# A three-layer graph network on one core: the slot table scattered three columns a step, and the first weights rounded earlier

## Chip, cores and metric

One core of a Trainium2 chip. The metric is the device time of one execution in microseconds (us); lower is better. Engines: PE (TensorE), DVE (VectorE), ACT (ScalarE), POOL (GpSimd) and SP (SyncE, which here only issues DMAs).

## The reference, cut to what matters

```python
x = x + gnn(layernorm(x), src, dst)       # x is 10000 x 512 f32, 10000 edges sorted by dst
x = x + ffn(layernorm(x))                 # 8 experts of 64 hidden columns, top 2
# gnn, three times:
h_neigh = segment_sum(h[src], dst) / max(deg, 1)
h = relu(h @ W_self[l] + h_neigh @ W_neigh[l] + b[l]);  h = h / |h|
```

## The kernel before, in words

All products are done with both factors split into two float16 parts (high and low, three matmuls for each pair of 128-blocks; `products`, L487). A weight matrix is rounded once: ACT writes the high part (`weight_hi`, L835), DVE the low part (`weight_lo`, L1095). Both need the matrix's scale, which comes from column norms (`square_sums` on PE, `weight_norm` and `weight_scale` on DVE, `largest_norm` on POOL).

**The first layer** goes over the 10000 nodes in their own order, in 79 tiles of 128. For tile t: SP loads x (L551); DVE takes mean and variance (`stats0`); POOL raises the variance to -1/2 (`dev0`, L674); DVE normalises (`norm0`, L1224); ACT and DVE make the high and low parts (`hi0`, `lo0`); PE turns the tile (`turn`); ACT copies it from PSUM (`turn0`, L871, HT); PE multiplies by the neighbour weights (`neigh`, psY) and by the own weights (`own`, psS); ACT and DVE write the first result as two halves (`yhi`, `ylo`), DVE adds the bias to the second (`sev`); SP stores both (L562, L564), 256 KB each. The second and third layers go over 79 tiles of edges instead and need tables: for each slot (tile, column) the node that it belongs to.

**The order of work.** Every engine runs its own list of steps. `run_plan` (L117) goes through the steps; in each, first the jobs that are set to this step run, then the stages in the order listed, each on tile step + offset. A stage with offset 4 works four tiles ahead. POOL's stage is `dev0` with offset 4, so in step s it serves tile s + 4. PE's stages are `neigh` at 0, `turn` at 1 and `own` at 0, and `own(t)` waits until `sev(t-1)` has emptied the accumulator. ACT's are `hi0` at 2, `yhi` at 0, `turn0` at 1; so `turn0` of tile t stands behind `hi0` of tile t + 1, and PE's tile t waits for the power of tile t + 1. DVE's are `sev` at -1, `norm0` at 2, `stats0` at 4, `lo0` at 2, `ylo` at 0.

**The tables** are made beside this as jobs. In steps 4 to 23 POOL scatters the node table, four columns a step. DVE works out each node's slot (to step 46). **From step 48 on POOL scatters the slot table in DRAM**: 80 columns, each an indirect DMA that writes 125 rows of 8 bytes (`columns`, L650, the DMA at L653), four a step in steps 48 to 67, each step's after `dev0`. Columns of even and odd steps count on two semaphores, s_scat0 and s_scat1, 16 for each column that has landed. Before a step's columns, POOL waits until those of two steps before have landed (`slot_columns`, L692). In step 68 `slot_columns_done` (L702) waits for all and loads the table back (L705), ahead of that step's `dev0`. DVE copies it in step 71 (`slot_table_loaded`, L1297), PE turns it in step 72 (`turn_slots`, L1627), DVE makes the index tables in step 73 (`tables`, L1302, s_tables at its end). After the first layer POOL and PE wait for s_tables, and POOL for the landing of all rows stored, before the gathers of the second layer start (`gather`, L728).

**The first weights.** Matrix 0 (n0) is rounded on ACT and DVE in step -1, matrix 1 (s0) in step 0. SP's `load_weight(2)` and `load_weight(3)` (L501, steps -1 and 0) wait for the low parts of 0 and 1.

Of the kernel before, what the change touches and what calls it, by code (L numbers as in the profile page):

```python
# [26 lines left out]
NP_, NF = 80, N // 80  # L27
# [5 lines left out]
STEP_EDGES = 4  # L33
STEP_INFO = STEP_EDGES + 20
STEP_SLOTS = 28
STEP_SCATTER = 48
STEP_TABLES = 71
NODES_A_STEP = 7
X_RING = 4

# [1 line left out]
def WSTEP(m):  # L42

    return 2 + 4 * (m - N_FIRST) + (m == 6)
# [60 lines left out]
def run_steps(tiles, stages, begin, end, run=0):  # L105
    for step in range(begin, end):
        for off, f in stages:
            if 0 <= step + off < tiles:
                f(Tile(step + off, run))
# [6 lines left out]

def run_plan(tiles, stages, jobs, windows=()):  # L117
    offs = [o for o, _ in stages]
    begin, end = -max(max(offs), 0), tiles - min(min(offs), 0)
    cuts = sorted({begin, end} | {j[0] for j in jobs} | {e for w in windows for e in w[:2]})  # L120
    for a, b in zip(cuts, cuts[1:]):
        for at, f, arg in jobs:
            if at == a:
                f() if arg is None else f(arg)
        run_steps(tiles, stages + [(0, f) for x, y, f in windows if x <= a and b <= y], a, b)
# [105 lines left out]
def build(nc, x, src, dst, W_self, W_neigh, b, Wg, W1, b1, W2, b2, ln_g, ln_b, out_g, out_b, out):  # L231
    with ExitStack() as ctx:
# [6 lines left out]
        def sem(name):  # L239
            return ctx.enter_context(nc.semaphore(name))  # L240

        def dram(name, shape, dt):
            return nc.dram_tensor(name, shape, dt)
# [6 lines left out]
        table = dram("slot_table", [SLOTS, 2], F32)  # L250
# [122 lines left out]
        s_sc = [sem(f"s_scat{i}") for i in range(2)]  # L373
# [8 lines left out]
        def view(at, parts, n, dt=F32):  # L382
            v = area[0:parts, at:at + n]
            return v if dt is F32 else v.bitcast(dt)
# [19 lines left out]
        slotT = view(P * 9, P, 80, U32)  # L404
        ndT = view(P * 10, P, 160).rearrange("p (t two) -> p t two", two=2)
# [93 lines left out]
        def _(sp):  # L499
# [58 lines left out]
            def store(t):  # L558
# [5 lines left out]
                sp.dma_start(Sd0[bass.ds(t.t * P, rows), :], SB[t.slot(2)][0:rows, :]).then_inc(s.s2[t.slot(2)], 16)  # L564

            run_plan(TN, [(5, load_x), (-1, store)],
                     [(-2, small_loads, None), (-2, table_starts, None), (-1, load_weight, 2), (0, load_weight, 3)]
                     + [(WSTEP(m - 1) + 1, load_weight, m) for m in range(4, len(NAMES))])
# [47 lines left out]
        def _(pool):  # L616

            node_limit = pool.alloc_register("node_limit")
            slot_limit = pool.alloc_register("slot_limit")
# [30 lines left out]
            def columns(index, value, to, limit, rows, i, at, count):  # L650

                for k in range(at, at + count):
                    pool.indirect_dma_start(  # L653
                        to[:, :], bass.IndirectOffsetOnAxis(ap=index[0:rows, k:k + 1], axis=0),
                        value[0:rows, k, :], None, bounds_check=limit, oob_is_err=False).then_inc(s_sc[i], 16)
# [31 lines left out]
            def info_done():  # L687
                for i in range(2):
                    pool.wait_ge(s_sc[i], 640)
                pool.dma_start(nI, info.rearrange("(p k) two -> p k two", p=NP_)).then_inc(s_nload, 16)  # L690

            def slot_columns(t):  # L692

                g = t + -STEP_SCATTER
                i = t.slot(2)
                pool.wait_ge(s_sc[i], (g + -2).landed(2) * 4 + 640)
                columns(slotT, ndT, table, slot_limit, NF, i, g.t * 4, 4)

            def slot_columns_in():
                pool.wait_ge(s_scat_in, 2)  # L700

            def slot_columns_done():  # L702
                for i in range(2):
                    pool.wait_ge(s_sc[i], 1280)
                pool.dma_start(tI, table.rearrange("(p k) two -> p k two", p=T)).then_inc(s_tload, 16)  # L705

            run_plan(TN, [(4, dev0)],
                     [(WSTEP(m) + 2, largest_norm, m) for m in range(N_FIRST, len(NAMES))]
                     + [(STEP_GATE + 2, largest_norm, CG), (STEP_EDGES, edge_columns_in, None), (STEP_INFO, info_done, None),
                        (STEP_SCATTER, slot_columns_in, None), (STEP_SCATTER + 20, slot_columns_done, None)],  # L710
                     [(STEP_EDGES, STEP_INFO, info_columns), (STEP_SCATTER, STEP_SCATTER + 20, slot_columns)])
            pool.wait_ge(s_tables, 1)

            for l in (1, 2, 3):
# [3 lines left out]
                tiles = TN if l == 1 else T  # L718
# [99 lines left out]
        def _(act):  # L818
# [39 lines left out]
            def yhi(t, l):  # L858
                i = t.slot(2)
                s = ph[l]  # L860
                act.wait_ge(s.y, (t + 1).n)
                if t.t >= 2:
                    act.wait_ge(s.ys[i], (t + -2).landed(2))
                k = Y_LN / (WUP * LN_UP) if l == 0 else Y_H / (WUP * H_UP)
                act.activation(YB[i][:, 0:D], psY[i][:, :], ACT.Copy, scale=k).then_inc(s.yhi, 1)  # L865

            def turn0(t):
# [4 lines left out]

            rest = range(N_FIRST, len(NAMES))
            run_plan(TN, [(2, hi0), (0, lambda t: yhi(t, 0)), (1, turn0)],
                     [(-1, weight_hi, 0), (0, weight_hi, 1)] + [(WSTEP(m) + 4, weight_hi, m) for m in rest]
                     + [(WSTEP(m), squares, m) for m in rest] + [(STEP_GATE, gate_squares, None)])

            def carry_hi(t, l):
# [109 lines left out]
        def _(dve):  # L988
# [252 lines left out]
            def ylo(t, l):  # L1241
                s = ph[l]
                i = t.slot(2)
                dve.wait_ge(s.yhi, (t + 1).n)
                k = Y_LN / (WUP * LN_UP) if l == 0 else Y_H / (WUP * H_UP)
                dve.scalar_tensor_tensor(YB[i][:, D:2 * D], psY[i][:, :], k, YB[i][:, 0:D], ALU.mult, ALU.subtract  # L1246
                                         ).then_inc(s.ylo, 1)

            def sev(t, l):
                s = ph[l]  # L1250
                i = t.slot(2)
                dve.wait_ge(s.sp, (t + 1).n)
                if t.t >= 2:
                    dve.wait_ge(s.s2[i], (t + -2).landed(2))
                c = C[f"s{l}"]
                dve.scalar_tensor_tensor(SB[i][:, :], psS[i][:, :], downs[:, c:c + 1], bias[:, l, :],  # L1256
                                         ALU.mult, ALU.add).then_inc(s.sev, 1)
# [44 lines left out]
            def tables():  # L1302
# [6 lines left out]
                for l in range(LAYERS):  # L1309
# [6 lines left out]
            rest = range(N_FIRST, len(NAMES))  # L1316
            run_plan(TN,
                     [(-1, lambda t: sev(t, 0)), (2, norm0), (4, stats0), (2, lo0), (0, lambda t: ylo(t, 0))],
                     [(-3, weight_norm, 1), (-2, weight_scale, 1), (-1, weight_lo, 0), (0, weight_lo, 1),
                      (0, self_down, None), (1, bias_columns, None), (1, edges, None), (3, edges_turned, None)]  # L1320
                     + [(WSTEP(m) + 2, weight_norm, m) for m in rest] + [(WSTEP(m) + 3, weight_scale, m) for m in rest]
                     + [(WSTEP(m) + 5, weight_lo, m) for m in rest]
# [6 lines left out]
                        (STEP_SLOTS, node_ranks, None), (STEP_SLOTS + FREE_STEPS, slots_by_node, None),  # L1329
                        (STEP_SCATTER - 1, slots_turned, None), (STEP_TABLES, slot_table_loaded, None),  # L1330
                        (STEP_TABLES + 2, tables, None)],
                     [(STEP_SLOTS, STEP_SLOTS + FREE_STEPS, free_slots)])
# [236 lines left out]
        def _(pe):  # L1569
# [96 lines left out]
            def own(t, l):  # L1666
# [3 lines left out]
                if l == 0 and t.t == 0:  # L1670
# [6 lines left out]
                        (STEP_SLOTS - 1, counts_before, None), (STEP_SCATTER - 2, turn_nodes, None),  # L1677
                        (STEP_TABLES + 1, turn_slots, None)])

# [116 lines left out]
```

## Time and profile before

| | |
|---|---|
| median of 3 runs | 2206.17 us (2205.99 to 2208.15) |
| profiled execution | 2204.11 us, its span 2202.1 us |
| PE busy | 2037.8 us, 93% of the span |
| DVE, ACT, POOL busy | 1721.8, 994.8, 1262.6 us |
| granted TensorE clock, mean | 0.968 of full |
| first layer | to about 533 us of the span |

The span runs from the first instruction to the last. The profiled execution took 2.0 us more than its span, and is 2.1 us below the median. In the rows, times count from the span's start. "idle 1.31 <-DMA x" says that the engine sat idle for 1.31 us before the instruction and that the end of this was set by the DMA x. "issue" means that nothing that the profile shows was waited for.

### The profile page before, as it was taken

How to read it: one execution, taken by the hardware profiler on the slowest of the kernel's cores; microseconds unless marked ns; L12 is line 12 of the kernel's file. 1: busy time of each engine (PE TensorE's matmuls, PEld its weight loads, DVE VectorE, ACT ScalarE, POOL GpSimd, SP SyncE). 2: the span in 40 equal slices, each digit the busy share in tenths (PEclk: the TensorE clock that was granted, in tenths of full speed). 3: DMA queues.
4: the chain of work that ended last, by engine and by line, in shares of the span. 5: the costliest groups of instructions: out<-in, count | busy, mean ns of one | idle time of the engine just before them, and what ended most of it. 6: DMA issues, size and time to landing. Idle time of an engine off the chain costs nothing.

```text
span 2202.1 us, 43921 instructions
## 1 busy us (share of the span) xinstructions
PE 2037.8 (93%) x15309; PEld 1138.2 (52%) x15315; DVE 1721.8 (78%) x4122; ACT 994.8 (45%) x1699; POOL 1262.6 (57%) x1396
## 2 busy tenths in 40 slices
PE   6999999877999999997999999997399999999997
PEld 2444444333444444443444444443077777777775
DVE  7768985444788888885888888885589999999984
ACT  4444333223333433442333433443566666766741
POOL 2784127752566665553444444443668888888854
PEclk9999999998999999998999999998599999999998
DMA  6664349863555555553666666664668888888853
GB/s 203 165 162 132 130 135 130 103 103 98 163 173 174 174 174 174 175 175 134 200 216 219 216 219 218 218 218 164 169 146 173 181 173 176 178 176 172 177 88 43
DMA packets 246210, 364.12 MB, mean 165 GB/s; under 512 B 115578, under 2 KB 115752, under 8 KB 245992
## 3 DMA queue, kind: packets, MB, share of 16 engines
q1 hardware_dynamic: 185175, 195.88, 35.0%
q0 software_dynamic: 60816, 165.43, 28.8%
q8 instruction: 125, 2.05, 0.4%
q14 instruction: 94, 0.76, 0.1%
HBM read 175.81 MB, written 165.31 MB: 155 GB/s over the span
## 4 chain that ended last, share of the span: by engine, by line
PE 74%; POOL 7%; DVE 6%; issue 5%; DMA 3%; ACT 3%; SPq 0%; DVEq 0%; POOLq 0%; ACTq 0%
PE psS L492 29%; PE psY L492 23%; PE psY L1730 10%; POOL slot_table L653 4%; PE psT L1654 4%; PE psA L1698 2%; PE psA L1699 2%; POOL node_info L653 2%; PE psS L1754 1%; DMA slot_table<-area 1%; DVE R L1364 1%; DVE area L1408 1%; PE psY L1732 1%; PE psA L1764 1%; POOL scl L674 1%
## 5 line engine op out<-in xcount | busy, mean ns | idle before, releaser
L492 PE MATMUL psY<-w_n,HT 128*128 128x512 f16 x2844 | 663.8, 384 | 45.4 <-ACT HT L871 43.1
L492 PE MATMUL psS<-w_s,HT 128*128 128x512 f16 x2844 | 652.6, 379 | 0.0
L492 PEld LDWEIGHTS psY<-w_n,HT 128*128 128x128 f16 x2844 | 278.3, 99 | 394.8 <-ACT HT L871 55.1
L492 PEld LDWEIGHTS psS<-w_s,HT 128*128 128x128 f16 x2844 | 268.3, 98 | 280.5
L898 ACT ACTIVATE RR<-R 128x512 f32<-128x512 f32 x237 | 149.5, 631 | 362.5 <-DVE R L1364 362.5
L757 POOL DMA_INDIRECT y_rows<-YB,poutT x158 | 160.4, 1015 | 188.2 <-DVE YB L1246 159.9
L750 POOL TENSOR_TENSOR scl<-ssm,halfpow 128x1 f32<-128x1 f32 x158 | 88.6, 560 | 247.7 <-DVE ssm L1382 247.7
L492 PE MATMUL psS<-w_w,raw 128*128 128x512 f16 x948 | 217.4, 379 | 0.0
L1256 DVE SCALAR_TENSOR_TENSOR SB<-psS,downs,bias 128x512 f32<-128x512 f32 x237 | 177.6, 749 | 47.5 <-PE psS L492 41.1
L1246 DVE SCALAR_TENSOR_TENSOR YB<-psY,YB 128x512 f16<-128x512 f32 x237 | 162.4, 685 | 36.5 <-ACT YB L865 36.1
L906 ACT ACTIVATE HH<-RR,scl 128x512 f16<-128x512 f32 x158 | 114.0, 722 | 148.7 <-POOL scl L750 148.7
L1364 DVE SCALAR_TENSOR_TENSOR R<-psA,invs,Sl 128x512 f32<-128x512 f32 x237 | 173.3, 731 | 9.8 <-ACT G L887 8.6
L728 POOL DMA_INDIRECT G<-y_rows,srcT x120 | 136.1, 1134 | 62.8 <-issue 31.4
L865 ACT ACTIVATE YB<-psY 128x512 f16<-128x512 f32 x237 | 137.8, 581 | 75.3 <-PE psY L492 56.1
L856 ACT ACTIVATE HH<-R 128x512 f16<-128x512 f32 x79 | 49.7, 630 | 269.2 <-DVE R L1224 267.3
L1654 PEld LDWEIGHTS psT<-iden,HH 128*128 128x128 f16 x1896 | 126.8, 98 | 67.6 <-ACT HH L906 7.1
L807 POOL DMA_INDIRECT out_dram<-raw,poutT x79 | 147.0, 1861 | 15.5 <-issue 14.3
L1654 PE MATMUL psT<-iden,HH 128*128 128x128 f16 x1896 | 146.1, 221 | 10.0 <-DVE HH L1231 4.6
L674 POOL TENSOR_TENSOR scl<-ssm,halfpow 128x1 f32<-128x1 f32 x79 | 62.2, 789 | 160.7 <-DVE ssm L1217 155.1
L492 PEld LDWEIGHTS psS<-w_w,raw 128*128 128x128 f16 x948 | 91.6, 97 | 109.2
L728 POOL DMA_INDIRECT area<-y_rows,srcT x117 | 123.3, 1054 | 30.8 <-issue 30.8
L1349 DVE SCALAR_TENSOR_TENSOR G<-psA,G 1x512 f16<-1x512 f32 x78 | 52.9, 679 | 93.7 <-ACT G L887 93.7
(280 smaller groups left out, 3657.0 us busy)
## 6 DMA issues: line engine op xcount, KB each, us to landing
self_rows<-SB SPq DMA_DIRECT2D x236, 256.0 KB, 2.0
Sl<-self_rows SPq DMA_DIRECT2D x158, 256.0 KB, 3.9
area<-in_x_dram SPq DMA_DIRECT2D x78, 256.0 KB, 4.8
y_rows<-YB SPq DMA_DIRECT2D x78, 256.0 KB, 4.3
out_dram<-obb SPq DMA_DIRECT2D x78, 256.0 KB, 4.2
raw<-in_L_gnn_W_neigh_dram SPq DMA_DIRECT2D x12, 256.0 KB
raw<-in_L_gnn_W_self_dram SPq DMA_DIRECT2D x12, 256.0 KB, 4.2
y_rows<-YB,poutT POOLq DMA_INDIRECT x158, 3.0
```

Of the source, the lines that this page charges most:

```text
L492: mm = eng.matmul(acc, lhs[:, a, c, :], w[:, bpart, c, :], start=(n == 0), stop=(stop and n == 3 * KC - 1))
L653: pool.indirect_dma_start(to[:, :], bass.IndirectOffsetOnAxis(ap=index[0:rows, k:k + 1], axis=0), value[0:rows, k, :], None, bounds_check= ...
L728: pool.indirect_dma_start(G[i][:, :], None, Yd[l - 1][:, :], bass.IndirectOffsetOnAxis(ap=srcT[:, t.t:t.t + 1], axis=0), bounds_check=node ...
L757: pool.indirect_dma_start(Yd[l][:, :], bass.IndirectOffsetOnAxis(ap=poutT[:, t.t:t.t + 1], axis=0), YB[i][:, :], None, bounds_check=node_l ...
L807: pool.indirect_dma_start(out[:, :], bass.IndirectOffsetOnAxis(ap=poutT[:, t.t:t.t + 1], axis=0), OUT[i], None, bounds_check=node_limit, o ...
L865: act.activation(YB[i][:, 0:D], psY[i][:, :], ACT.Copy, scale=k).then_inc(s.yhi, 1)
L898: act.activation(RR[i][:, :], R[i][:, :], ACT.Relu).then_inc(s.rr, 1)
L1246: dve.scalar_tensor_tensor(YB[i][:, D:2 * D], psY[i][:, :], k, YB[i][:, 0:D], ALU.mult, ALU.subtract).then_inc(s.ylo, 1)
L1256: dve.scalar_tensor_tensor(SB[i][:, :], psS[i][:, :], downs[:, c:c + 1], bias[:, l, :], ALU.mult, ALU.add).then_inc(s.sev, 1)
L1364: dve.scalar_tensor_tensor(R[i][:, :], psA[0 if l == 3 else i][:, :], invs[:, l - 1, t.t:t.t + 1], Sl[i][:, :], ALU.mult, ALU.add).then_in ...
L1654: mm = pe.transpose(psT[i][:, a, c, :], HH[i][:, a, c * P:(c + 1) * P], iden16[:, :])
L1730: pe.matmul(psH[:, cols], w[:, bpart, c, cols], h[:, a, c, :], start=first, stop=False)
```

## The change

The slot table's columns go out three a step over 27 steps (48 to 74, two columns in the last) instead of four over 20. What POOL waits for before a step's columns is the same, those of two steps before. `slot_columns_done` moves from step 68 to 75, `slot_table_loaded` on DVE from 71 to 78, `turn_slots` on PE from 72 to 79, `tables` from 73 to 80. Step 79 is behind PE's last stage and step 80 behind DVE's, so `run_plan` now runs on until the last job. `weight_hi` of matrices 0 and 1 moves on ACT from steps -1 and 0 to -2 and -1, `weight_lo` of matrix 0 on DVE from step -1 to -2; that of matrix 1 stays in step 0.

```diff
-STEP_TABLES = 71
+SLOTS_A_STEP = 3
+SCATTER_STEPS = -(-80 // SLOTS_A_STEP)
+STEP_TABLES = 78
...
 def run_plan(tiles, stages, jobs, windows=()):
     offs = [o for o, _ in stages]
-    begin, end = -max(max(offs), 0), tiles - min(min(offs), 0)
+    begin, end = -max(max(offs), 0), max([tiles - min(min(offs), 0)] + [j[0] + 1 for j in jobs])
...
+            def slots_sent(g):
+
+                return sum(min(SLOTS_A_STEP, 80 - SLOTS_A_STEP * k) for k in range(g % 2, g, 2))
+
             def slot_columns(t):
 
-                g = t + -STEP_SCATTER
-                i = t.slot(2)
-                pool.wait_ge(s_sc[i], (g + -2).landed(2) * 4 + 640)
-                columns(slotT, ndT, table, slot_limit, NF, i, g.t * 4, 4)
+                g = (t + -STEP_SCATTER).t
+                at = g * SLOTS_A_STEP
+                pool.wait_ge(s_sc[g % 2], 640 + 16 * slots_sent(g))
+                columns(slotT, ndT, table, slot_limit, NF, g % 2, at, min(SLOTS_A_STEP, 80 - at))
...
             def slot_columns_done():
                 for i in range(2):
-                    pool.wait_ge(s_sc[i], 1280)
+                    pool.wait_ge(s_sc[i], 640 + 16 * slots_sent(SCATTER_STEPS + (SCATTER_STEPS + i) % 2))
                 pool.dma_start(tI, table.rearrange("(p k) two -> p k two", p=T)).then_inc(s_tload, 16)
...
-                        (STEP_SCATTER, slot_columns_in, None), (STEP_SCATTER + 20, slot_columns_done, None)],
-                     [(STEP_EDGES, STEP_INFO, info_columns), (STEP_SCATTER, STEP_SCATTER + 20, slot_columns)])
+                        (STEP_SCATTER, slot_columns_in, None), (STEP_SCATTER + SCATTER_STEPS, slot_columns_done, None)],
+                     [(STEP_EDGES, STEP_INFO, info_columns), (STEP_SCATTER, STEP_SCATTER + SCATTER_STEPS, slot_columns)])
...
-                     [(-1, weight_hi, 0), (0, weight_hi, 1)] + [(WSTEP(m) + 4, weight_hi, m) for m in rest]
+                     [(-2, weight_hi, 0), (-1, weight_hi, 1)] + [(WSTEP(m) + 4, weight_hi, m) for m in rest]
...
-                     [(-3, weight_norm, 1), (-2, weight_scale, 1), (-1, weight_lo, 0), (0, weight_lo, 1),
+                     [(-3, weight_norm, 1), (-2, weight_scale, 1), (-2, weight_lo, 0), (0, weight_lo, 1),
```

## Rows read from the trace of the kernel before

**Rows 1.** The page: the chain that ended last, shares of the span by line

```profile
PE psS L492 29%; PE psY L492 23%; PE psY L1730 10%; POOL slot_table L653 4%; PE psT L1654 4%; PE psA L1698 2%; PE psA L1699 2%; POOL node_info L653 2%; PE psS L1754 1%; DMA slot_table<-area 1%; DVE R L1364 1%; DVE area L1408 1%; PE psY L1732 1%; PE psA L1764 1%; POOL scl L674 1%
```

**Rows 2.** Busy time of each engine by stage, clock, DMA share, GB/s

```profile
core 0: us, PE busy (x) PEld busy (x) DVE busy (x) ACT busy (x) POOL busy (x), PEclk, DMA share, GB/s
324.80:372.10 47.30, 47.12 (x266) 22.97 (x264) 27.66 (x56) 16.33 (x24) 33.35 (x30) 1.00 1.05 126
372.10:431.50 59.40, 47.40 (x253) 21.95 (x252) 25.98 (x54) 15.65 (x23) 44.63 (x40) 0.94 0.83 108
478.00:481.50 3.50, 0.00 (x0) 0.00 (x0) 0.00 (x0) 0.00 (x0) 0.00 (x0) 0.63 0.00 0
```

**Rows 3.** PE in order of time, tiles 48, 49, 71 and 72

```profile
321.16 2.75 PE L492 MATMUL psY<-w_n,HT 128*128 128x512 f16 x12
326.79 2.75 PE L492 MATMUL psY<-w_n,HT 128*128 128x512 f16 x12
...
485.46 4.57 PE L492 MATMUL psY<-w_n,HT 128*128 128x512 f16 x12 [9.68 <-ACT HT L871]
...
493.05 2.75 PE L492 MATMUL psY<-w_n,HT 128*128 128x512 f16 x12
```

**Rows 4.** POOL in order of time: a power, one whole step

```profile
323.70 0.89 POOL L674 TENSOR_TENSOR scl<-ssm,halfpow 128x1 f32<-128x1 f32 x1 [5.13 <-issue]
...
431.52 1.47 POOL L653 DMA_INDIRECT slot_table<-area  x1 [0.22 <-issue]
...
434.88 1.19 POOL L653 DMA_INDIRECT slot_table<-area  x1 [0.30 <-issue]
436.37 1.19 POOL L653 DMA_INDIRECT slot_table<-area  x1 [0.30 <-issue]
...
438.37 1.47 POOL L653 DMA_INDIRECT slot_table<-area  x1 [0.21 <-issue]
```

**Rows 5.** Last columns and what waits for them, POOL; totals for slot_table

```profile
329.56 1.32 POOL L653 DMA_INDIRECT slot_table<-area  x1 [0.30 <-issue]
...
339.31 1.24 POOL L653 DMA_INDIRECT slot_table<-area  x1 [1.31 <-DMA slot_table<-area]
...
372.10 1.23 POOL L653 DMA_INDIRECT slot_table<-area  x1 [1.55 <-DMA slot_table<-area]
...
472.34 1.19 POOL L653 DMA_INDIRECT slot_table<-area  x1 [0.30 <-issue]
481.54 0.62 POOL L705 DMA_DIRECT2D area<-slot_table  x1 [8.01 <-DMA slot_table<-area]
482.17 1.20 POOL L674 TENSOR_TENSOR scl<-ssm,halfpow 128x1 f32<-128x1 f32 x2
...
  DMA slot_table<-area: 18.5, 8
...
DMA to landing us min/median/max: 2.2/2.2/2.2
```

**Rows 6.** DVE's tables, and the end of the first layer

```profile
497.07 0.23 DVE L1304 COPY area<-psA 128x79 f32<-128x79 f32 x1
...
499.70 0.15 DVE L1313 TENSOR_SCALAR small<-ones 128x1 f32<-128x1 f32 x1
...
532.19 0.75 DVE L1256 SCALAR_TENSOR_TENSOR SB<-psS,downs,bias 128x512 f32<-128x512 f32 x1 [1.27 <-PE psS L492]
...
535.42 1.13 POOL L728 DMA_INDIRECT G<-y_rows,srcT  x1 [27.68 <-DMA self_rows<-SB]
```

**Rows 7.** The first weights and the first tiles, all engines

```profile
18.48 0.63 ACT L856 ACTIVATE HH<-R 128x512 f16<-128x512 f32 x1 [5.01 <-DVE R L1224]
...
21.12 2.35 DVE L1099 SCALAR_TENSOR_TENSOR w_n<-raw,ups,w_n 128x2048 f16<-128x2048 f32 x1 [1.05 <-ACT w_n L837]
...
27.51 2.35 DVE L1099 SCALAR_TENSOR_TENSOR w_s<-raw,ups,w_s 128x2048 f16<-128x2048 f32 x1 [1.95 <-ACT w_s L837]
...
39.15 2.77 PE L492 MATMUL psY<-w_n,HT 128*128 128x512 f16 x12 [0.38 <-ACT HT L871]
```

## The prediction

> **What bounds the kernel now.** Start with the page: PE is busy for 93% of the span, so most microseconds elsewhere are free. The chain of waits says where they are not. Besides the two products of L492, it holds 4% of POOL's slot_table scatter and 1% of DMA slot_table<-area [rows 1], and both lie between 324 and 482 us. Next the table of stages [rows 2]. From 324.8 to 372.1, in the scatter's first steps, PE is still busy for 47.1 of 47.3 us; from 372.1 to 431.5 PE works 47.4 of 59.4 us, and POOL 44.6. There PE waits, and POOL is the engine to look at.
>
> PE's order of time gives the size [rows 3]. A tile that nothing holds takes 326.79 - 321.16 = 5.63 us. Tile 48 starts at 321.16 and tile 72 at 493.05: 171.9 us for 24 tiles where 24 x 5.63 = 135.1 would do. **The excess is 36.8 us**, and it is all that the scatter's part of the change can give back. It includes the gap of 9.68 us ahead of tile 71, and that tile's first product at a lower clock (4.57 us, where tile 72's took 2.75).
>
> POOL's order of time gives the cause [rows 4]. A step of POOL is one small power (L674, which norm0 waits for) and then four columns. Where nothing holds it, it lasts 438.37 - 431.52 = 6.85 us, more than PE's 5.63. It also waits for the columns of two steps before to land: 8 waits, 18.5 us in all, 8.0 of them in the one ahead of the table's reading, behind which the next powers queue [rows 5]. Power of tile 52 starts at 323.70 and that of tile 72 at 482.17: 158.5 us for 20 steps, 45.9 more than 20 x 5.63. PE feels 36.8 of these. So the first **9.1 us of POOL's lag are free**: power t is issued about three tiles before PE needs it.
>
> **Part 1, three columns a step.** One column less is 436.37 - 434.88 = 1.49 us less, so an unhindered step of POOL falls from 6.85 to 5.36 us, under PE's 5.63. As many columns and powers are issued as before. What is left is the landing wait, and it gets tighter. I measure it by the distance d from the start of a group's last column to the start of the next column of the same parity. With four columns, POOL's own pace leaves 2 x 6.85 - 4.85 = 8.85 us for it (4.85 = 436.37 - 431.52); with three at PE's pace it leaves 2 x 5.63 - 3.36 = 7.90 us. Where the wait binds, two steps last 3.36 + d, so a step lasts p = (3.36 + d) / 2.
>
> What d is, before shows in part [rows 5]. While PE ran at full pace, between 339.31 and 372.10, four steps lasted 32.8 us, 8.20 each, so d = 2 x 8.20 - 4.85 = 11.55; the first group's was 9.75 (329.56 to 339.31). Late, POOL went on without a landing wait (431.52 and 438.37 [rows 4]), so d was at most the 8.85 of its own pace. After the last column it was 9.2 (472.34 to 481.54). I take 11.5 for the first quarter of the groups, where PE's pace and the addresses are the same as before, and 8.5 for the rest, between the 7.90 at which the wait vanishes and the 9.2 of the last group. The mean is 9.25, which makes **p = 6.3 us**. The ends: p = 5.63 if d stays under 7.90, and p = 6.65 if the rest has 9.2 and a third of the groups 11.5 (mean 9.95).
>
> The powers of tiles 52 to 78 are 26 steps apart. POOL's lag is 26 x (6.3 - 5.63) = 17.4 us, less 9.1 free: an excess of 8.3 in place of 36.8, **28.5 us less**. The ends are 36.8 less (p up to 5.98), and 26 x 1.02 - 9.1 = 17.4 left over, so 19.4 less.
>
> The Trainium skill, "DMA: Bandwidth & Descriptors", section "Anatomy of one DMA — SWDGE (gpsimd) path", gives a DMA issued by GpSimd about 2.0 us plus its bytes at 436 KB per us. By it, a column of 1 KB would have d near 3.3 us with its issue, no wait would be left, and the sum would be that of the first rival. The trace disagrees: 9.2 us, though the DMA engines moved nothing between 478.0 and 481.5 [rows 2, 5].
>
> **Part 2, the table read in step 75 instead of 68.** The wait of 8.0 us ahead of L705 no longer has a power behind it: tile 78's is issued in step 74, and POOL has nothing more to do in this layer. Its cost is new at the far end. In step 78 DVE waits for the loaded table (L1298) ahead of sev(77), and PE's own(78) waits for that. Count from D, the start of power 78. In before, power 72 started at 482.17 and tile 71 on PE at 485.46 [rows 3, 5], so tile 77 starts at D + 3.3, tile 78 at D + 8.9, and own(78) is due 2.6 later at D + 11.5. The last two columns start at D + 0.8 and D + 2.6; with d = 9.2 the reading starts at D + 11.8 and lands 2.2 us later [rows 5]; the two copies and sev(77) add 1.2 [rows 6]: D + 15.2, which is 3.7 us late. With d = 7.3 it is 1.8 late, and it is nothing if POOL has no lag. I take **2.5 us more**.
>
> The last step's tables (L1304 to L1313) took 497.07 to 499.85, 2.8 us beside PE's work. Now they stand behind sev(78), which ended at 532.94, so they end at about 535.7, and POOL's first gather, which started at 535.42 when self_rows had landed [rows 6], starts some 0.3 us after that. **0.6 us more.** The transposes of L1630 and L1631 take 0.3 us at the end of PE's queue and are in this.
>
> **Part 3, first weights sooner.** ACT sat idle for 5.0 us until 18.48, with n0's scale already worked out (that is DVE's work ahead of its step -4), and rounded w_n only behind hi0(0). In step -2 its 2 us fall into that gap and cost nothing. DVE sat idle for 1.05 and 1.95 us ahead of its two products of L1099, each time for ACT [rows 7]. Now the first can start at 18.0, ahead of norm0(0), which it pushes back by 2.35 us; w_s on ACT follows right behind hi0(0), and DVE is done with both at about 27.1 instead of 29.86. PE's first tile moves little, since it waits for the pushed norm0; its third had waited for HT behind DVE (39.15) and could now start at 37.8, right after own(1). SP is released for its loads of matrices 2 and 3 some 3 us sooner, between its first loads of x. I take **1.4 us less**; the ends are 2.5 less (all of DVE's lead) and 0.5 more (the loads meet x's, or the pushed norm0 counts). It stays if nothing later was waiting for something else.
>
> **Sum** against the profiled execution: -36.8 + 8.3 + 2.5 + 0.6 - 1.4 = -26.8, from 2204.1 (span 2202.1) to 2177.3. The median of the runs is 2206.2, 2.1 above, so I forecast **2179.4**. The later layers have the same instructions; I give them nothing.
>
> **Rivals.** *Full saving.* With fewer columns in flight d stays under 8.6 on average (p under 5.98): no excess. -36.8 + 0.6 - 1.4 = -37.6, 2168.6. For it: late groups needed no wait at 8.85, with two columns more in flight [rows 4]. Against it: d = 11.5 at exactly the pace that PE would return to.
>
> *Crowded queue, slower than before.* From 324.8 to 372.1 the DMA engines were busy for 1.05 of the time, later, at the slower pace, for 0.83 [rows 2]. If the tiles' own 256 KB stores at 5.6 to 7 us a tile hold the small columns up everywhere as they did there, d stays at 11.55, p = 7.46, and the excess is 26 x 1.83 - 9.1 = 38.5; the read table comes 6.0 us late by the reckoning of part 2. -36.8 + 38.5 + 6.0 + 0.6 - 1.4 = +6.9: 2213. It decides from p = 7.2, a mean d of 11.0. Against it: PE then slows to the same p and leaves room, as it did after 372.
>
> The Trainium skill, same page, section "Queues, rings and completion order", states that the semaphore's write lands only after every earlier write of that DMA engine, across its queues. That is this rival's mechanism; the rows can't tell it from plain queueing.
>
> *Half given back.* p between 6.65 and 7.1: 2191 to 2203.
>
> *The change does nothing.* The saving is taken by what is late next (ACT's wait for y_rows stores, DVE's for self_rows), which PE's own pace would bring back; this is p near 7.2 by another way.
>
> **Chances.** Forecast (p 5.98 to 6.65, 2169 to 2191) 0.58; full saving 0.22; half given back 0.11; no difference 0.04; crowded 0.05. A measurement of this kernel tells 0.2%, 4.4 us, from no change: faster 0.91, same 0.04, slower 0.05. The range from 2167.5 (full saving with the better end of part 3) to 2192 leaves under 2 in 10 out.
>
> **What the changed profile would show.** Three columns and a power about 6.3 us apart, waits for slot_table landings in more than half of the steps, longest early; PE's gaps ahead of psY under 1 us a tile, no lowered clock between 372 and 500; L705 near 498 with a long wait and no power behind it; DVE's L1299 ahead of the last sev, L1304 to L1313 after the last one; gather about 26 us sooner. I am wrong if POOL's steps are 5.63 (full saving), 7.2 or more (crowded), or if PE waits there for another releaser than ACT's HT behind a power.

## The result, and the profile after

| | before | changed |
|---|---|---|
| median | 2207.16 us, 4 runs (2205.99 to 2210.55) | 2181.74 us, 4 runs (2179.51 to 2184.16) |
| profiled execution | 2204.11 us, span 2202.1 | 2180.63 us, span 2178.5 |
| PE busy | 2037.8 us | 2035.9 us |

The changed kernel takes 0.9869 of the time before, interval 0.9847 to 0.9891: 25.4 us less by the medians, 23.6 by the two spans. The forecast was 2179.4, with 2167.5 to 2192 as its range. One execution of the kernel before in the third set below took 10858 us and is in no comparison.

First the page of the changed kernel, its chain that ended last by line. Line numbers have moved: L655 scatters, L676 is the power, L711 reads the table, L494 multiplies, L877 copies HT, L1105 rounds low parts.

```profile
PE psS L494 29%; PE psY L494 23%; PE psY L1736 10%; PE psT L1660 4%; POOL slot_table L655 3%; PE psA L1704 2%; PE psA L1705 2%; POOL node_info L655 2%; PE psS L1760 1%; DMA slot_table<-area 1%; DVE R L1370 1%; DVE area L1414 1%; PE psY L1738 1%; PE psA L1770 1%; POOL scl L676 1%
```

The scatter is still in it, 3% where it had 4% [rows 1]. Next the table of stages of the changed kernel, over its scatter (columns as in [rows 2]).

```profile
324.00:372.00 48.00, 48.00 (x277) 23.97 (x276) 28.39 (x58) 17.40 (x25) 29.87 (x27) 1.00 0.97 135
372.00:431.00 59.00, 54.01 (x303) 26.01 (x301) 32.29 (x65) 20.17 (x29) 40.01 (x38) 1.00 0.96 124
431.00:496.00 65.00, 61.38 (x340) 29.56 (x339) 35.28 (x70) 22.55 (x33) 47.33 (x44) 0.97 0.77 117
```

From 372 to 431 PE now works 54.0 of 59.0 us, where it had 47.4 of 59.4, and the clock stays at 1.00 there. PE's order of time gives the size as before [rows 3]. These are tiles 48 and 57, the tile behind the longest gap, and tile 78.

```profile
321.65 2.75 PE L494 MATMUL psY<-w_n,HT 128*128 128x512 f16 x12
...
373.29 2.76 PE L494 MATMUL psY<-w_n,HT 128*128 128x512 f16 x12 [0.84 <-ACT HT L877]
...
448.87 4.44 PE L494 MATMUL psY<-w_n,HT 128*128 128x512 f16 x12 [2.52 <-ACT HT L877]
...
502.10 2.75 PE L494 MATMUL psY<-w_n,HT 128*128 128x512 f16 x12
```

Tile 48 starts at 321.65, 0.5 later than before, and tile 78 at 502.10, where before had 526.80. At 5.627 us a tile the 30 tiles between would take 168.8; they take 180.5. **The excess is 11.7 us, where it was 36.8.** Seven gaps ahead of psY, all behind 372 and all for HT, make 8.6 us of it (0.84, 0.95, 1.10, 2.10, 0.52, 2.52, 0.58). Of the other 3.1 us, 1.7 are the clock: the product behind the longest gap took 4.44 us, not 2.75, and the granted clock of the last stage is 0.97. About 1.2 are 0.17 us beside each gap.

POOL's order of time in the changed kernel shows why some is left:

```profile
324.20 0.89 POOL L676 TENSOR_TENSOR scl<-ssm,halfpow 128x1 f32<-128x1 f32 x1 [5.13 <-issue]
...
339.35 1.24 POOL L655 DMA_INDIRECT slot_table<-area  x1 [2.99 <-DMA slot_table<-area]
340.90 1.20 POOL L655 DMA_INDIRECT slot_table<-area  x1 [0.30 <-issue]
342.40 1.19 POOL L655 DMA_INDIRECT slot_table<-area  x1 [0.30 <-issue]
...
369.28 1.23 POOL L655 DMA_INDIRECT slot_table<-area  x1 [5.84 <-DMA slot_table<-area]
...
446.38 1.47 POOL L655 DMA_INDIRECT slot_table<-area  x1 [0.21 <-issue]
...
451.76 1.47 POOL L655 DMA_INDIRECT slot_table<-area  x1 [0.21 <-issue]
...
492.56 0.59 POOL L676 TENSOR_TENSOR scl<-ssm,halfpow 128x1 f32<-128x1 f32 x1
...
495.14 1.20 POOL L655 DMA_INDIRECT slot_table<-area  x1 [0.30 <-issue]
500.96 0.63 POOL L711 DMA_DIRECT2D area<-slot_table  x1 [4.62 <-DMA slot_table<-area]
```

An unhindered step takes 451.76 - 446.38 = 5.38 us, shorter than PE's 5.63. But the powers of tiles 52 and 78 stand 492.56 - 324.20 = 168.4 us apart, 6.48 a step. The difference is waiting for columns to land, which the view of the tile slot_table sums up:

```profile
  DMA slot_table<-area: 39.7, 16
...
  POOL slot_table L655: 35.1, 15
  POOL area L711: 4.6, 1
```

Before, it was 18.5 us in 8 waits [rows 5]. POOL waited more for columns and PE less for POOL, because POOL's own work fell from 6.85 to 5.38 us a step.

Last, DVE and POOL at the end of the layer:

```profile
503.78 0.22 DVE L1305 COPY area<-area 79x128 f32<-79x128 f32 x1 [3.19 <-DMA area<-slot_table]
...
504.18 0.74 DVE L1262 SCALAR_TENSOR_TENSOR SB<-psS,downs,bias 128x512 f32<-128x512 f32 x1
...
510.77 0.15 DVE L1319 TENSOR_SCALAR small<-ones 128x1 f32<-128x1 f32 x1
...
511.21 1.14 POOL L734 DMA_INDIRECT G<-y_rows,srcT  x1 [9.62 <-DVE small L1319]
```

The first gather starts at 511.21, before at 535.42 [rows 6]: 24.2 us sooner, against 23.6 for the span. So nothing of weight changed behind the first layer.

### The profile page after: what moved, and what is told of

It reads as the page before. It is cut to its first block, busy times and chain, and to the rows that moved or that the text cites. A ratio compares the mean times of both kernels' runs of the same rounds, so it can differ in the third digit from the quotient of the medians.

```text
span 2178.5 us, 43921 instructions
## 1 busy us (share of the span) xinstructions
PE 2035.9 (93%) x15309; PEld 1139.4 (52%) x15315; DVE 1722.8 (79%) x4122; ACT 995.7 (46%) x1699; POOL 1264.7 (58%) x1396
## 4 chain that ended last, share of the span: by engine, by line
PE 74%; DVE 7%; POOL 7%; issue 5%; ACT 3%; DMA 3%; SPq 0%; DVEq 0%; POOLq 0%; ACTq 0%
PE psS L494 29%; PE psY L494 23%; PE psY L1736 10%; PE psT L1660 4%; POOL slot_table L655 3%; PE psA L1704 2%; PE psA L1705 2%; POOL node_info L655 2%; PE psS L1760 1%; DMA slot_table<-area 1%; DVE R L1370 1%; DVE area L1414 1%; PE psY L1738 1%; PE psA L1770 1%; POOL scl L676 1%
## 5 line engine op out<-in xcount | busy, mean ns | idle before, releaser
L494 PE MATMUL psY<-w_n,HT 128*128 128x512 f16 x2844 | 662.8, 383 | 22.0 <-ACT HT L877 19.9
L494 PE MATMUL psS<-w_s,HT 128*128 128x512 f16 x2844 | 652.5, 379 | 0.0
L494 PEld LDWEIGHTS psY<-w_n,HT 128*128 128x128 f16 x2844 | 279.0, 99 | 368.8 <-ACT HT L877 27.6
L494 PEld LDWEIGHTS psS<-w_s,HT 128*128 128x128 f16 x2844 | 268.5, 98 | 280.3
L494 PE MATMUL psS<-w_w,raw 128*128 128x512 f16 x948 | 217.4, 379 | 0.0
L1252 DVE SCALAR_TENSOR_TENSOR YB<-psY,YB 128x512 f16<-128x512 f32 x237 | 162.4, 685 | 29.4 <-ACT YB L871 29.2
L494 PEld LDWEIGHTS psS<-w_w,raw 128*128 128x128 f16 x948 | 91.6, 97 | 109.2
L676 POOL TENSOR_TENSOR scl<-ssm,halfpow 128x1 f32<-128x1 f32 x79 | 60.4, 765 | 142.8 <-DVE ssm L1223 137.0
L655 POOL DMA_INDIRECT slot_table<-area x80 | 100.8, 1260 | 54.2 <-DMA slot_table<-area 35.1
```

The source lines that it names most:

```text
L494: mm = eng.matmul(acc, lhs[:, a, c, :], w[:, bpart, c, :], start=(n == 0), stop=(stop and n == 3 * KC - 1))
L655: pool.indirect_dma_start(to[:, :], bass.IndirectOffsetOnAxis(ap=index[0:rows, k:k + 1], axis=0), value[0:rows, k, :], None, bounds_check= ...
```

## The experiments

They ran in three sets, each on a chip of its own, beside runs of the kernel before on the same chip. There it took 2197.4, 2197.3 and 2199.4 us (medians), 8 to 10 us less than where the result was measured. Ratios are against the same set. "Excess" is always the start of tile 78 less that of tile 48, less 168.8 us. How late columns land is given as the mean, over the steps of one profiled execution, of the time from the start of a step's last column to its landing.

**Weights sooner, alone** (the kernel before with part 3 only).

```diff
-                     [(-1, weight_hi, 0), (0, weight_hi, 1)] + ...
+                     [(-2, weight_hi, 0), (-1, weight_hi, 1)] + ...
-                     [(-3, weight_norm, 1), (-2, weight_scale, 1), (-1, weight_lo, 0), (0, weight_lo, 1),
+                     [(-3, weight_norm, 1), (-2, weight_scale, 1), (-2, weight_lo, 0), (0, weight_lo, 1),
```

> The kernel before with only the first weights rounded sooner (part 3 alone). By the forecast's term 1.4 us less than before, 2205.8. If the lead is lost on the way to the scatter, within 0.5 us of before, 2207, with tile 48 between 321.2 and 321.7 although tile 2 starts near 38.1.

Measured: 2198.28 us in 12 runs, ratio 1.0004 (0.9993 to 1.0014). **Part 3 brings nothing that can be measured**: at most 1.5 us of gain, at most 3.1 of loss.

**The changed kernel without it.** The same edit reversed.

> The changed kernel with the first weights rounded in their old steps (part 3 undone). The step table says that part 3 is worth 1.4 us: 2183.1. The traces of before and after say otherwise: tile 2 starts 1.0 us sooner, but tile 48 starts 0.5 us later (321.16 and 321.65), so by them part 3 is worth nothing that lasts: 2181 to 2182, with tile 48 at about 321.2.

Measured: 2169.99 us, ratio 0.9868 (0.9852 to 0.9885), excess 0.0. The changed kernel itself had 0.9853 (below); the intervals overlap, so this says only that parts 1 and 2 carry the gain. The start of tile 2 on PE shows what part 3 does, in this kernel and in the changed one, both in order of time:

```profile
40.08 2.75 PE L494 MATMUL psY<-w_n,HT 128*128 128x512 f16 x12
```

```profile
38.14 2.75 PE L494 MATMUL psY<-w_n,HT 128*128 128x512 f16 x12
```

The lead is there at tile 2 and all but gone by tile 48: 322.83 without part 3, 321.65 and 321.59 with it in two profiles of the changed kernel, but 320.13 with part 3 alone and 318.78 in a profile of the kernel before in the third set. Profiled executions differ by more than the lead.

**The late read, alone** (four columns a step as before, but the table read in step 75, copied in 78).

```diff
-STEP_TABLES = 71
+STEP_TABLES = 78
...
-                        (STEP_SCATTER, slot_columns_in, None), (STEP_SCATTER + 20, slot_columns_done, None)],
+                        (STEP_SCATTER, slot_columns_in, None), (STEP_TABLES - 3, slot_columns_done, None)],
```

> Four columns a step over 20 steps as before, but the wait for all of them and the table's reading moved to step 75 (and the tables to steps 78 to 80). Theory A, the number of columns a step is what counts: the 8.0 us wait goes and with it the gap of 9.7 us and the low clock behind it, POOL's steps stay at 7.5 us, so 9 to 12 us less than before, 2195 to 2198. Theory B, the blocked power behind the final wait is what mattered and three columns do little: within 3 us of the changed kernel, 2182 to 2185.

Measured: 2187.77 us, ratio 0.9954 (0.9941 to 0.9966): 10 us less, as theory A had it. PE's tiles 48 and 78:

```profile
322.63 2.75 PE L492 MATMUL psY<-w_n,HT 128*128 128x512 f16 x12
...
509.34 2.75 PE L492 MATMUL psY<-w_n,HT 128*128 128x512 f16 x12
```

The excess is 17.9 us; with part 3 alone, in the same set, it was 30.3. So the wait ahead of the read, with the gap and the lower clock behind it, cost about 12 us, and the long steps of four columns the other 18. With three columns on top (the run without part 3 above) the time falls from 2187.77 to 2169.99, 17.8 us. Both halves of the change work; three columns with the early read were not run.

**The changed kernel again**, in the second set.

> The changed kernel once more, as the control of this set, since the first set ran at 2197.4 us for the kernel before where the forecast's chip ran at 2207.2. There, with the old weights, the changed kernel had no excess at all between tiles 48 and 78 (mean d of 8.6 us, 19.8 us of landing waits). If d is what decides: on a chip with mean d up to 8.6 us the excess is 0 to 2 us and the ratio to before about 0.986 to 0.987; on one with mean d near 9.8 us about 12 us of excess are left.

Measured: 2166.77 us, ratio 0.9853 (0.9837 to 0.987). Within the intervals this is the ratio of the first chip, by another way. Its POOL waits, and PE's tiles 48 and 78:

```profile
  DMA slot_table<-area: 16.7, 14
...
  POOL slot_table L655: 14.1, 13
  POOL area L711: 2.6, 1
```

```profile
321.59 2.75 PE L494 MATMUL psY<-w_n,HT 128*128 128x512 f16 x12
...
490.39 2.75 PE L494 MATMUL psY<-w_n,HT 128*128 128x512 f16 x12
```

**No excess is left**: the outcome of the rival "full saving". By the landing events of the trace, a group's last column lands 7.5 us after its start in the mean, where the first profile of the changed kernel has 8.9. The mean d is 8.4 here and 9.84 there, and 8.6 was the bound below which POOL's lag stays within the free 9.1 us.

**The kernel before again**, in the third set, whole.

> The kernel before once more, for its trace on the chip of this set: it gives the excess that there was to win. If the ratio of the changed kernel is the same on both kinds of chip (0.987 and 0.985) only because less is to be won where all of it is won, the excess between tiles 48 and 78 is here 28 to 32 us (36.9 on the forecast's chip) and the mean landing latency shorter than there. If it is 36.9 us here, too, the rest of the kernel moved instead.

Measured: 2198.18 us, ratio to its set's other runs 0.9995 (0.9985 to 1.0006), so the comparison itself is good to 0.15%. Its excess is 29.4 us (tile 48 at 318.78, tile 78 at 517.01), where it was 36.8; its waits for columns are 10.3 us, where they were 18.5; its columns land 7.5 us after their start, where it was 8.6. So on these chips there was less to gain and less was left: 29.4 in this profile and 0.0 in that of the changed kernel in the second set, against 36.8 and 11.7. Why the landings are quicker there stays open.

**Three groups in turn** (columns wait for those of three steps before, so that up to nine are in flight; three runs of it, one in each set).

```diff
-                return sum(min(SLOTS_A_STEP, 80 - SLOTS_A_STEP * k) for k in range(g % 2, g, 2))
+                return sum(min(SLOTS_A_STEP, 80 - SLOTS_A_STEP * k) for k in range(g % 3, g, 3))
...
-                pool.wait_ge(s_sc[g % 2], 640 + 16 * slots_sent(g))
-                columns(slotT, ndT, table, slot_limit, NF, g % 2, at, min(SLOTS_A_STEP, 80 - at))
+                after(pool, s_slot[g % 3], 16 * slots_sent(g))
+                columns(slotT, ndT, table, slot_limit, NF, g % 3, at, min(SLOTS_A_STEP, 80 - at), s_slot)
...
```

> The changed kernel, but with three semaphores in turn, so that POOL waits for the columns of three steps before (up to nine columns in flight, not six). Theory A, the rest of the excess (11.7 us between tiles 48 and 78) is the landing wait's distance d against 7.9 us: a wait now needs d over 13.5, so nearly all of it goes: 2170 to 2173. Theory C, the DMA engines are saturated by tile rows and columns together, and more in flight only land later: 2180 to 2183, POOL's waits about as long in total (39.7 us).

> Three semaphores in turn once more, beside the changed kernel on the same chip. No landing wait and no excess on either kind of chip. So 0 to 2 us less than the changed kernel where that has a mean d up to 8.6 us, and 9 to 12 us less where that still has its excess.

> Three semaphores in turn a third time. If this chip is like the second set's (before at 2197), as there: 2166, no excess. If it is like the forecast's (before at 2207), the changed kernel has 11.7 us of excess there, and this one should have 0 to 2 us and a ratio of 0.981 to 0.983 to before, against 0.987 of the changed kernel.

Measured: 2166.99, 2166.31 and 2167.84 us, ratios 0.9859, 0.9860 and 0.9850, with half widths of 0.0015 to 0.0018. The waits between columns are gone and the excess is 0.7, 0.0 and 0.0; in the third set one is left, ahead of the read:

```profile
  DMA slot_table<-area: 3.1, 1
  POOL area L712: 3.1, 1
```

The time is that of the changed kernel (2166.77 beside 2166.31 in one set), since no excess was left there to take. The columns do land later with up to nine in flight, 8.8, 8.5 and 8.9 us, where six had 7.5: that half of theory C holds. No wait comes of it, since a wait would need a d over 13.5. What three groups do where 11.7 us are left wasn't seen: no set fell on such a chip.

**One group in flight** (the columns wait for those of the step before as well).

```diff
                 pool.wait_ge(s_sc[g % 2], 640 + 16 * slots_sent(g))
+                pool.wait_ge(s_sc[(g + 1) % 2], 640 + 16 * slots_sent(g + 1))
```

> The changed kernel, but before each step's columns POOL waits for those of the step before, too (one group of three in flight). A step must then last 3.36 us plus d. If d is a latency of its own, 6 to 7.5 us even with little in flight, the steps last 9.4 to 10.9 us, and the time grows by 26 x (9.4 to 10.9 less 5.63) - 9.1 = 89 to 128 us over a kernel with no excess. If d is only a queue of columns, it falls to about 3 us, the steps to 6.4, and the time grows by 10 to 15 us.

Measured: 2244.6 us in 2 runs, ratio 1.0212 (1.0191 to 1.0232), 78 us over the changed kernel of the set. That is below the 89 to 128 us expected of a latency and far above the 10 to 15 of a queue alone. POOL's waits, and PE's tiles 48, 72 and 78:

```profile
  DMA slot_table<-area: 106.0, 25
```

```profile
319.20 2.75 PE L494 MATMUL psY<-w_n,HT 128*128 128x512 f16 x12
...
518.47 4.45 PE L494 MATMUL psY<-w_n,HT 128*128 128x512 f16 x12 [3.55 <-ACT HT L878]
...
564.08 2.75 PE L494 MATMUL psY<-w_n,HT 128*128 128x512 f16 x12
```

The last column stands 560.2 - 322.9 = 237.3 us after the first, 9.1 a step, and the excess is 76.1 us. By the prediction's way of counting that is 26 x (9.1 - 5.63) - 9.1 = 81 us. So the wait for landings alone sets the step once it binds, and PE feels nearly all of it. A column lands in 5.1 us in the mean here, with three in flight and PE slow, and in 7.5 with six at full pace: landing gets longer with what is in flight. Whether that traffic is the tiles' rows or the columns themselves, the last three runs ask.

**Small stores of the tiles' rows** (from tile 46 on; the rows left out are filled before the scatter begins).

```diff
+                if t.t >= 46:
+                    rows = 1
                 sp.dma_start(Sd0[bass.ds(t.t * P, rows), :], SB[t.slot(2)][0:rows, :]).then_inc(s.s2[t.slot(2)], 16)
...
```

> The changed kernel, but from tile 46 on the stores of self_rows move one row instead of 128 (a third of the tile's DMA bytes is left out in the scatter's steps; those rows were filled with the output bias in steps 30 to 40, so the result of the layer is not computed). If the columns land late because they queue with the tile rows, the mean d falls by 1 us or more and the landing waits to below half of the changed kernel's. If a column's own 125 small writes set d, it stays within 0.3 us and the waits too.

Measured: 2164.96 us, ratio 0.9853 (0.9836 to 0.9869). The stages of this kernel, and then those of the changed one in the same set:

```profile
324.00:372.00 48.00, 48.00 (x271) 23.73 (x270) 30.31 (x60) 17.76 (x25) 37.36 (x34) 1.00 0.66 94
372.00:431.00 59.00, 59.00 (x340) 29.42 (x339) 37.05 (x73) 22.92 (x32) 44.03 (x40) 1.00 0.72 94
```

```profile
324.00:372.00 48.00, 48.00 (x277) 23.95 (x276) 29.20 (x58) 18.64 (x26) 38.18 (x35) 1.00 0.85 136
372.00:431.00 59.00, 59.00 (x334) 29.24 (x333) 36.80 (x76) 22.04 (x31) 44.11 (x40) 1.00 0.98 145
```

A third of the bytes is gone, the DMA engines fall from 0.98 to 0.72, and the columns still take 7.2 us to land (7.5 with all rows), the mean d is 8.6 (8.4) and POOL still waits 18.4 us (16.7). **This third of the tiles' rows doesn't set the landing.** The other two thirds, the loads of x and the stores of y_rows, were not taken away.

**Wide rows** (each column writes rows of 256 bytes, not 8, into a table of that pitch; the same with three groups). The table's first fill now writes separate pieces of 8 bytes, and SP reads the table back in step 76, in such pieces too.

```diff
-        table = dram("slot_table", [SLOTS, 2], F32)
+        table = dram("slot_table", [SLOTS, WIDE], F32)
...
-                        value[0:rows, k, :], None, bounds_check=limit, oob_is_err=False).then_inc(s_sc[i], 16)
+                        value[0:rows, k, :] if to is info else area[0:rows, P * 10 + 2 * k:P * 10 + 2 * k + WIDE], None, bounds_check=limit, oob_is_err=False).then_inc(s_sc[i], 16)
```

> The changed kernel with columns of 125 rows of 256 bytes instead of 8 (the table is wider; only its first two words are used and read back, by SP at step 76, so the table comes some us later at the layer's end). If longer landings are what leaves an excess, d grows (to 9.8 us or more, if 32 KB beside the tiles' 768 KB weigh) and an excess of 26 x ((3.36 + d) / 2 - 5.63) - 9 to 10 us appears between tiles 48 and 78: 9 us at d = 9.8. If the count of small writes sets d and not their bytes, d and the excess (0) stay.

> The same wide columns with three semaphores in turn. If the excess of the wide kernel comes from the landing wait, it is gone here (0 to 2 us), as long as d stays under 13.5 us. If it comes from saturated DMA engines that hold the tile rows, it is as large as with two groups or larger.

Measured: 2332.7 and 2332.3 us, ratios 1.0600 and 1.0601. That is no price of the scatter. SP's load behind the table's fill was held for 117.5 us, and its store behind the table's reading for 59.0; ACT waited for that store, and PE for ACT, 49.6 us ahead of tile 78. The two together, 167 us, are about the 166 us by which this kernel is slower than the changed kernel of the second set. In order of time, SP at the fill, SP behind the reading, and PE:

```profile
15.59 0.86 SPq L560 DMA_DIRECT2D slot_table<-area  x1
16.49 117.50 SPq L555 DMA_DIRECT2D area<-in_x_dram  x1
...
588.76 59.02 SPq L566 DMA_DIRECT2D y_rows<-YB  x1
...
651.19 5.09 PE L496 MATMUL psY<-w_n,HT 128*128 128x512 f16 x12 [49.58 <-ACT HT L883]
```

That gap is all of the excess, so the excess tells nothing of the scatter here. The scatter itself is the finding, and against both expectations. Between its columns there is no landing wait (one of 1.7 us stands ahead of the reading), and the stages show PE at full pace with the DMA engines half idle, for more bytes per us than the changed kernel moved:

```profile
  issue: 22.3, 80
```

```profile
480.00:520.00 40.00, 40.00 (x233) 20.02 (x232) 24.79 (x51) 15.14 (x22) 33.87 (x30) 1.00 0.53 159
520.00:584.00 64.00, 64.00 (x367) 31.80 (x365) 38.78 (x79) 24.90 (x35) 54.08 (x46) 1.00 0.49 146
```

Columns land in 2.9 to 4.0 us, 3.5 in the mean. The tiles' rows gain too, as the DMA view of 120 us of the scatter shows, first with wide rows, then with 8 bytes:

```profile
q1 hardware_dynamic: 9309, 16.97, 43.5%
...
y_rows<-YB SPq DMA_DIRECT2D x21, 256.0 KB, 2.0
```

```profile
q1 hardware_dynamic: 9029, 16.45, 89.4%
...
y_rows<-YB SPq DMA_DIRECT2D x22, 256.0 KB, 7.8
```

As many bytes of the tiles' rows keep the engines busy for half the time and land in 2.0 us instead of 7.8. The two kernels ran on different chips, but three groups with 8 bytes on the chip of the wide rows had columns landing in 8.9 us and a DMA share of 0.97 and 0.94 in the first two stages. So rows of 8 bytes in a pitch of 8 make both late. The pitch of the table changed with the rows' size, and the runs don't tell which of the two is the reason.

## Why the prediction was right

The mechanism of part 1 held: POOL's step fell under PE's, and what excess was left came of the landing wait. The sum of -26.8 came out as -24.2 at the first gather and -23.6 in the span. Part of that closeness is luck: three of its terms were off by 1.9 to 3.4 us, and the errors (+3.4, -2.5 and +1.9) cancel in part.

- **An excess of 36.8 to give back.** Right in what it consists of, POOL's steps and the read: in the first set 12 of 30 us were the read's, 18 the steps'.
- **An unhindered step of 5.36.** Measured 5.38.
- **p = (3.36 + d) / 2.** Right in form. Where a group has waited, its first column is shorter (1.24 and not 1.47 us), so that the group takes 342.40 - 339.35 = 3.05, not 3.36. With the measured mean of 9.84 for d that gives 6.45, and the powers show 6.48.
- **PE's gaps under 1 us, no lowered clock.** Not quite: three gaps of seven were longer (1.10, 2.10, 2.52), and one product ran at the low clock.
- **8.3 us of excess left.** Too low: 11.7. The step that failed is "8.5 for the rest": d stayed long in the later groups too, 9.84 in the mean where 9.25 was taken. The bound of 8.85 came from two late groups [rows 4], which weren't typical: by the same trace the distances behind the first five run from 8.8 to 12.8 us. Whether d depends on PE's pace isn't shown; in the second set it was 8.4 with PE at full pace all the time.
- **The reading 2.5 us late.** It cost nothing. D, the start of power 78, is 492.56. The reading started at D + 8.4 (500.96), not D + 11.8, because the last d was 500.96 - 495.14 = 5.8 us and not 9.2, with five columns in flight and not eight. Tile 78 started at D + 9.5, not D + 8.9, and own(78) right behind its first product, at 504.69 by PE's order of time. The prediction had put "nothing if POOL has no lag" as an end; here POOL kept a lag and the short last d did it. The term of 2.5 was for a delay that never came.
- **The tables 0.6 late.** From sev(78) on, the gather stands 511.21 - 504.69 = 6.5 us behind own(78), 6.0 before: 0.5. Right.
- **Weights 1.4 us sooner.** Wrong. Tile 2 started 1.0 us sooner (38.14 against 39.15), a tile near 225 us still 0.5 (224.67 against 225.21), tile 48 0.5 later. "It stays if nothing later was waiting for something else" was the condition that failed: on the way PE waits for HT again and again (2.04 us ahead of 81.46, 2.28 ahead of 224.67, 3.21 ahead of 251.04), and the low clock falls on other products, 4.37 us for the one at 251.04, where before had 4.24 for the one at 225.21. Part 3 alone measures as nothing.

In the sum: -36.8 + 11.7 + 0 + 0.5 + 0.5 = -24.1 (the last 0.5 is tile 48's later start).

Of the rivals, "full saving" is what the later chips did, with a mean d of 8.4 in the second set, under the 8.6 set as its condition (8.62 in the run without part 3). "Crowded queue" did not come, and its cause gets no support: with a third of the tiles' bytes gone the landing stays.

The rule cited from the Trainium skill, "DMA: Bandwidth & Descriptors", section "Anatomy of one DMA — SWDGE (gpsimd) path", 2.0 us and the bytes, has the columns land far too soon here (7.5 to 8.9 us); it is nearer with wide rows, 2.9 to 4.0. The rule of order of the Trainium skill, same page, section "Queues, rings and completion order", that the semaphore's write comes behind all earlier writes of a DMA engine, would let 8-byte writes delay the tiles' rows as well as the columns, which is what is seen, but no run separates it from plain queueing. Nor did a run have 8-byte rows in a table of a wider pitch.

## What to carry to other kernels

When an engine off the path feeds the one on it, compare its step, unhindered, with the bound engine's step: a job of fixed total that is spread over more steps costs nothing once the step is the shorter one, and what waits for its completion belongs behind the last thing that others need from that engine. What then remains is latency, so count in one formula how far apart issue and wait stand; and expect that latency to differ from chip to chip (7.5 against 8.9 us here), so that 1.3 and 1.5% are won from different sums. A lead won at the start of a stage is worth only what survives the next wait for another engine.

## What the runs showed of the hardware

- Rows of 8 bytes, scattered into an 8-byte pitch, land later and cost the DMA engines more than rows of 256 bytes at a pitch of 256: 7.5 against 3.5 us for a column, a DMA share of 0.82 to 0.98 against about 0.5, and SP's 256 KB stores of y_rows land in 7.8 against 2.0 us.
- A step's last column of 8-byte rows lands, on the later chips, in 5.1 us with three in flight, 7.5 with six and 8.5 to 8.9 with up to nine. In the first of these PE, and with it the tiles' traffic, was slower too.
- A fill of the table in separate pieces of 8 bytes (10112 of them) held SP's next load for 117.5 us, where behind the same bytes in one run for each partition it took 1.5 us (changed kernel, second set). A reading in as many pieces held SP's next store for 59.0 us.
- The same kernel, that before the change, has column landings of 7.5 us in a profile on one chip and 8.6 on another, and 9 us between its medians.
